# Turning row maxima and expert tokens in 32 x 32 squares on DVE, with transfers that put the squares in place

## The chip, the cores and the metric
The kernel runs on one core of a Trainium2 chip. The metric is the device time of one execution in microseconds. A run is told as the time of that core; where a profile is read, its span is the time from the first to the last instruction that the profiler saw. Before: 1392.12 us, median of 3 runs (1388.15 to 1392.15).

## The reference
One layer on a sequence of S = 2048 rows of width D = 128: a layer norm without gain, attention with 16 heads of width 64, and a mixture of 8 experts of which each token uses one. Everything is float32; Wq, Wk, Wv and Wo are drawn 8 times larger than usual, so the scores are large and the row maxima must really be subtracted.

```python
xn = layernorm(x)                                   # (1, 2048, 128)
q, k, v = xn @ Wq, xn @ Wk, xn @ Wv                 # 16 heads of 64
scores = einsum('bqhd,bkhd->bhqk', q, k) * 64**-0.5
attn = softmax(scores, axis=-1)
a = einsum('bhqk,bkhd->bqhd', attn, v).reshape(1, 2048, 1024) @ Wo + bo
expert = argmax(softmax(xn @ router_w.T))           # one of 8 for each token
h = square(relu(xn @ expert_fc[expert]))            # 128 -> 512
f = h @ expert_proj[expert].T                       # 512 -> 128
out = x + a + f
```

## The kernel before, in words
**Blocks.** The heads are taken in 8 pairs (h = 0, 1), the queries in 4 chunks of 512. A pair and a chunk make a block n, 32 in all. In a block the loop runs over 16 key tiles kt of 128. For each kt and head PE makes a scores tile of 128 keys x 512 queries in one of three PSUM banks SB: a high product (`high_scores`, L1062) and a low product on top of it (`low_scores`, L1069). Queries and keys are split in a rounded high part and the rest, so K1/Q1 hold one set of parts and K2/Q2 another. ACT takes the exponential of the tile (L619), POOL and DVE add the tiles up for the denominators (L505, L790), and PE multiplies them with V in batches of 8 key tiles (`times_v`, L1116), after kt 8 of the same block and after kt 0 of the next.

**The row maxima.** The scores tile has keys on the partitions, so a query's maximum can't be subtracted there as a per-partition number. It goes in as one more row of the product: K2 holds a row of ones at partition 64 (head 0) or 0 (head 1), and Q2 holds minus the maximum of each query at that row. The maxima come from a second set of products, queries x keys, in three PSUM banks MB (`max_unit`, L1088; 32 units for a block), each reduced by DVE over 512 keys (`maxima`, L767). They run ahead of their block: at kt 11 of block n the last unit of block n + 1 is done. DVE then reduces 4 key chunks to one and negates (`minus_max`, L779) into `nm`, 128 x 8: partition = query in its tile of 128, column = head and query tile. At kt 12 (`AT_T`) PE turns `nm` into the spare PSUM bank XB (`turn_max`, L1169), ACT copies the 8 x 128 result to `mrow` (L653), and SP copies 4 rows per head into the row of Q2 (`place_max`, DMAs from L365). The first low product of block n + 1 (kt 0, head 0) waits for this on the semaphore `d_nm`.

**The expert tokens.** Early blocks sort the tokens by expert into the DRAM tensor `sorted_x`, in 23 tiles of 128 rows. Blocks 4 to 26 do one tile each. SP loads `tok` and two weight matrices at the end of the block before (`load_tile`, L416 to L418). At kt 3 PE turns `tok` (L1037), ACT copies it to `tokT` (L697), at kt 4 PE makes the first product (`expert_up`, L1043), at kt 11 the second (L1050).

**Order.** Each engine's program is written out by hand: the same two nested loops (blocks, kt) on every engine, in which the constants `AT_...` say at which kt a job stands. Engines run their programs in order and meet in semaphores. The spare bank XB is shared by all small PE jobs in turn: `take_spare` makes each wait until the one before it was read out. All DMAs but the indirect ones are issued by SP, in its own order: in a block the K pieces (two sets of 6, in blocks n with n % 4 < 2 and n < 28; "K work"), the Q pieces (6), then `place_max`, the store of an expert result (L423) and `load_tile`. K work is also a product, an ACT copy and, for K, a DVE subtraction (`low_k`, L903) at kt 1 and 9.

Of the kernel before, what the change touches and what calls it, by code (L numbers as in the profile page):

```python
# [30 lines left out]
P = 128  # L31
# [52 lines left out]


LEAD = 8
UNITS = 2 * TB * JB
# [17 lines left out]
def layer(nc, x, wq, wk, wv, wo, bo, router_wT, fc, projT, out):  # L105


    with ExitStack() as ctx:
# [3 lines left out]
        def sem(name):  # L112
            return ctx.enter_context(nc.semaphore(name))

        def bank(name, n=1):
# [48 lines left out]
        on = osb  # L164
        mx, nm = sb("mx", [P, 2, UNITS]), sb("nm", [P, 2, 2 * TB])
        mrow = sb("mrow", [2 * TB, P], F32R)
        MB_all, SB_all = bank("MB", 3), bank("SB", 3)
# [4 lines left out]

        t_s, t_m, t_pv, t_q, t_k, t_v, t_den, t_wo, t_nm = (
            sem(f"t_{n}") for n in ("s", "m", "pv", "q", "k", "v", "den", "wo", "nm"))

        a_e, a_o, a_q, a_k, a_w, a_v, a_nm, a_den = (
            [sem("a_e0"), sem("a_e1")], *(sem(f"a_{n}") for n in ("o", "q", "k", "w", "v", "nm", "den")))

        v_m, v_nm, v_q, v_k, v_w, v_rd, v_y = (
            sem(f"v_{n}") for n in ("m", "nm", "q", "k", "w", "rd", "y"))  # L180

# [13 lines left out]

        d_tile, t_tok, t_up, t_down, a_tok, a_up, a_res, g_hid, d_res, d_back, v_back = (
            sem(n_) for n_ in ("d_tile", "t_tok", "t_up", "t_down", "a_tok", "a_up", "a_res", "g_hid", "d_res",
                               "d_back", "v_back"))
# [5 lines left out]
        d_out = sem("d_out")  # L204
        QD, KD = 6 * 16, 6 * 16

# [142 lines left out]
        with nc.Block() as block:  # L349
            @block.sync  # L350
            def _(sp):
# [53 lines left out]
                def place_max(m):  # L405
                    k = m % QS
                    wait(sp, a_nm, m.times(1, 1))
                    wait(sp, g_z, 4 + 2 * QS if m.off else 4)
                    for h in range(2):
                        copy(Q2[k][h][maxrow[h], :], mrow[h * TB:(h + 1) * TB, :], d_nm[k])  # L410

                def load_tile(r):


                    e = sp.value_load(owner_i[0:1, bass.ds(r.place(1), 1)], min_val=0, max_val=E - 1)
                    sp.dma_start(tok[:, :], sorted_x[bass.ds(r.place(P), P), :]).then_inc(d_tile, 16)  # L416
# [79 lines left out]
            def _(pool):  # L496
# [46 lines left out]
                def first():  # L543
# [10 lines left out]
                                       base=0, pattern=[[1, P]], channel_multiplier=-1)  # L554
                    pool.memset(one_e[:, :], 1.0)
                    pool.memset(gate[:, :, 1:NT], 1.0)
                    pool.memset(gate[:, :, 0:1], 0.0)
# [53 lines left out]
            def _(act):  # L611
# [35 lines left out]

                def max_rows(m):
                    wait(act, t_nm, m.times(1, 1))
                    if not (m.i is None and m.off == 0):  # L650
                        old = m - 1
                        wait(act, d_nm[old % QS], (old // QS).times(32, 32))
                    act.activation(mrow[:, :], XB[0:2 * TB, 0:P], ACT.Copy).then_inc(a_nm, 1)  # L653

                def take_o(n):
# [38 lines left out]

                def copy_tokens(r):
                    wait(act, t_tok, r.times(1, 1))
                    act.activation(tokT[:, :], XB[:, 0:P], ACT.Copy).then_inc(a_tok, 1)  # L697

                def rectify(r):
# [8 lines left out]
                def first():  # L708
                    act.wait_ge(g_i, 2)
                    act.activation(up[:, 0:1], eps[:, 0:1], ACT.Sqrt)  # L710

                    root(0)
                    split_w(Lin(0))
                    root(1)
                    turned(0)
                    turned(1)
                    root(2)
                    root(3)
                    high_q0()
                    high_k0(0)  # L720
                    high_k0(1)
                    for p in range(UNITS // 2):
                        kind, c = BETWEEN.get(p, (None, 0))
                        if kind == "t":
                            turned(c)
                            copy_k0(c - 2)
                        elif kind == "k":
                            high_k0(c)
                            copy_k0(c)
                        elif kind == "v":  # L730
                            kv("v", Lin(0), c)
                        elif kind == "q":
                            high_q(Lin(c))
                    max_rows(Lin(0))

                def one(n):
                    for kt in range(NT):
# [3 lines left out]
                        if has_tile(n):  # L741
                            if kt == AT_TOK:
                                copy_tokens(n - TILE0)
# [10 lines left out]
                        if kt == AT_DEN and not (n.i is None and n.off == 0):  # L754
                            take_sums(n - 1)
                        if kt == AT_T and before(n, NB - 1):
                            max_rows(n + 1)

# [3 lines left out]
            def _(dve):  # L762
# [13 lines left out]
                def minus_max(m):  # L776
                    wait(dve, v_m, m.times(UNITS, UNITS))
                    wait(dve, t_nm, m.times(1, -1))
                    dve.tensor_reduce(nm[:, m % 2, :], mx[:, m % 2, :].rearrange("p (a b) -> p a b", b=JB), AX.X,  # L779
                                      ALU.max, negate=True).then_inc(v_nm, 1)  # L780

                def add(n, kt):
# [102 lines left out]
                def find_owners():  # L885
# [3 lines left out]
                    dve.tensor_scalar(owner_i[:, :], owner[:, :], float(E - 1), None, ALU.min).then_inc(v_own, 1)  # L889

                def take_back(j):
                    dve.wait_ge(d_back, 16 * NT)
                    dve.wait_ge(v_y, NB - 2)
                    dve.tensor_tensor(chunk(Y, j), chunk(Y, j), chunk(back, j), ALU.add).then_inc(v_back, 1)
# [22 lines left out]
                def first():  # L917
# [17 lines left out]
                    for u in range(EARLY):  # L935
                        maxima(Lin(1), u)
                    choose()
                    for u in range(EARLY, MIDDLE):
                        maxima(Lin(1), u)

                def one(n):
                    start = n.i is None and n.off == 0
                    for kt in range(NT):
# [3 lines left out]
                        if kt == AT_NM and before(n, NB - 1):  # L947
                            minus_max(n + 1)
                        if kt in AT_KV and before(n, NB - JB):
                            kind, pair, c = kv_jobs(n)[AT_KV.index(kt)]  # L950
# [16 lines left out]
                        if n.off == NB - 1 and kt in BACK:  # L967
                            take_back(BACK[kt])
                        if kt == AT_WO:
                            if start:  # L970
# [28 lines left out]
            def _(pe):  # L999
# [165 lines left out]

                def turn_max(m):
                    take_spare(a_nm, m.times(1, 1))
                    wait(pe, v_nm, m.times(1, 1))
                    pe.transpose(XB[0:2 * TB, 0:P], nm[:, m % 2, :], ident[:, :]).then_inc(t_nm, 1)  # L1169

                def first():
# [22 lines left out]
                    for p in range(UNITS // 2):  # L1194
# [10 lines left out]
                        elif kind == "r":  # L1205
                            logits(c)
                    for u in range(EARLY):
                        max_unit(Lin(1), u)
                    turn_max(Lin(0))
                    for u in range(EARLY, MIDDLE):  # L1210
                        max_unit(Lin(1), u)
# [3 lines left out]
                def one(n):  # L1215
                    start = n.i is None and n.off == 0
                    for kt in range(NT):
# [8 lines left out]
                        if has_tile(n):  # L1226
                            if kt == AT_TOK:
                                turn_tokens(n - TILE0)
                            if kt == AT_UP:
# [7 lines left out]
                        if kt == AT_WO and not start:  # L1237
                            project(n - 1)
                        if kt == AT_T and before(n, NB - 1):
                            turn_max(n + 1)  # L1240
                        if kt == AT_DEN and not start:
# [45 lines left out]
```

## Time and profile before

| | |
|---|---|
| median of 3 runs | 1392.12 us (1388.15 to 1392.15) |
| the profiled execution | 1389.63 us |
| its span | 1387.9 us |
| mean granted TensorE clock | 0.993 |
| PE busy | 1365.8 us, 98% of the span |
| POOL busy | 1121.8 us, 81% |
| DVE busy | 1078.0 us, 78% |
| ACT busy | 735.2 us, 53% |

The profile comes from one execution. Busy time of PE counts a product from its issue to the modelled end in a pipeline, so two neighbours overlap: a 128 x 512 product has a duration of 0.39 us but the next one starts 0.23 us later. The chain of waits takes the overlap out and gives each its own share. SPq is the queue of SP: the time in which it issues a DMA. "Releaser" is the instruction or the DMA whose end lifted a wait.

### The profile page before, as it was taken

The numbers are of one execution on the slowest core, as the hardware profiler recorded it, in microseconds if no ns is written. First come the engines' busy times: TensorE is split into PE (matmuls) and PEld (weight loads), VectorE is DVE, ScalarE is ACT, GpSimd is POOL, SyncE is SP. The second block draws the span as 40 slices with busy tenths as digits, with TensorE's granted clock in tenths as the row PEclk, the third lists the DMA queues.
The fourth block names the chain that finished last, engine by engine and source line by source line (L and its number), as shares of the span: only waits on it lengthen the run. The fifth ranks groups of instructions, "written<-read, shape, count | busy, mean of one in ns | idle before, by whom it ended". The sixth has DMA issues, their size and how long they took to land.

```text
span 1387.9 us, 20006 instructions
## 1 busy us (share of the span) xinstructions
PE 1365.8 (98%) x6447; PEld 866.1 (62%) x6447; DVE 1078.0 (78%) x1468; ACT 735.2 (53%) x1316; POOL 1121.8 (81%) x908
## 2 busy tenths in 40 slices
PE   7899999999999999999999999999999999999997
PEld 4566666566665666666766666656667666656644
DVE  7987887786787767777777777778677777788877
ACT  4465455565464554554644645545546446556543
POOL 7779997777787877877878877879777788789995
PEclk8999999999999999999999999999999999999998
DMA  4241113220132201331113311123112231111000
GB/s 104 58 120 41 37 41 70 70 67 20 43 89 57 60 19 43 94 69 44 34 39 84 73 40 43 43 71 90 24 42 55 64 79 26 24 23 33 11 19 23
DMA packets 65255, 72.38 MB, mean 52 GB/s; under 512 B 9024, under 2 KB 38272, under 8 KB 65152
## 3 DMA queue, kind: packets, MB, share of 16 engines
q1 hardware_dynamic: 64128, 69.01, 20.3%
q0 software_dynamic: 1024, 2.10, 0.5%
q8 instruction: 52, 0.85, 0.2%
q14 instruction: 51, 0.42, 0.1%
HBM read 17.83 MB, written 5.11 MB: 17 GB/s over the span
## 4 chain that ended last, share of the span: by engine, by line
PE 93%; DVE 2%; POOL 1%; DMA 1%; issue 1%; SPq 1%; ACT 1%; POOLq 0%; DVEq 0%; ACTq 0%
PE OB L1116 31%; PE SB L1062 17%; PE SB L1069 16%; PE MB L1088 15%; PE XB L1153 2%; PE XB L1144 2%; PE XB L1162 2%; PE XB L1050 1%; PE XB L1043 1%; POOL acc L505 1%; DVE mx L767 1%; PE XB L1123 1%; PE XB L1125 1%; PE XB L1124 1%; DMA K<-low 1%
## 5 line engine op out<-in xcount | busy, mean ns | idle before, releaser
L505 POOL TENSOR_TENSOR acc<-acc,ex 128x512 f32<-128x512 f32 x717 | 915.9, 1304 | 99.9 <-DVE acc L790 40.4
L767 DVE TENSOR_REDUCE mx<-MB 128x1 f32<-128x512 f32 x992 | 655.9, 688 | 228.9 <-PE MB L1088 224.1
L619 ACT ACTIVATE ex<-SB 128x512 f32<-128x512 f32 x1024 | 607.2, 599 | 329.8 <-PE SB L1069 262.0
L1116 PE MATMUL OB<-ex,V 128*64 128x512 f32 x2048 | 452.7, 594 | 0.0
L1062 PE MATMUL SB<-Q,K 128*128 128x512 f32 x1024 | 421.9, 412 | 0.5 <-ACT ex L619 0.5
L1069 PE MATMUL SB<-Q,K 128*128 128x512 f32 x1024 | 399.8, 390 | 0.8 <-DMA Q<-mrow 0.8
L1088 PE MATMUL MB<-K,Q 128*128 128x512 f32 x992 | 389.1, 392 | 1.6 <-DVE mx L773 0.6
L1116 PEld LDWEIGHTS OB<-ex,V 128*64 128x64 f32 x2048 | 143.9, 137 | 284.3 <-issue 273.0
L1062 PEld LDWEIGHTS SB<-Q,K 128*128 128x128 f32 x1024 | 192.6, 188 | 96.5 <-issue 53.5
L790 DVE TENSOR_TENSOR acc<-acc,ex 128x512 f32<-128x512 f32 x179 | 205.0, 1145 | 13.5 <-ACT ex L619 1.0
L1088 PEld LDWEIGHTS MB<-K,Q 128*128 128x128 f32 x992 | 186.1, 188 | 46.7 <-DVE mx L767 5.0
L1069 PEld LDWEIGHTS SB<-Q,K 128*128 128x128 f32 x1024 | 193.1, 189 | 32.9 <-DMA Q<-mrow 1.2
L505 POOL TENSOR_TENSOR acc<-ex 128x512 f32<-128x512 f32 x63 | 79.8, 1287 | 137.6 <-ACT ex L619 137.5
L658 ACT ACTIVATE osb<-OB 128x512 f32<-128x512 f32 x32 | 19.1, 598 | 204.0 <-PE OB L1116 204.0
L908 DVE RECIPROCAL rd<-rd 128x256 f32<-128x256 f32 x62 | 104.1, 1720 | 0.0
L511 POOL TENSOR_TENSOR osb<-osb,rd 128x512 f32<-128x512 f32 x31 | 40.4, 1304 | 3.9 <-DVE rd L908 3.9
L898 DVE SCALAR_TENSOR_TENSOR low<-XB,high 128x512 fp32r<-128x512 f32 x31 | 21.4, 692 | 22.8 <-ACT high L633 22.8
L1144 PEld LDWEIGHTS XB<-wraw,xT 128*128 128x128 f32 x256 | 34.0, 195 | 3.5 <-issue 1.2
L1144 PE MATMUL XB<-wraw,xT 128*128 128x128 f32 x256 | 35.0, 281 | 0.0
L1162 PEld LDWEIGHTS XB<-wo,osb 128*128 128x128 f32 x248 | 32.4, 191 | 2.8 <-issue 0.4
L1153 PE MATMUL XB<-acc,ones 128*64 128x512 f32 x124 | 33.4, 618 | 0.0
L1162 PE MATMUL XB<-wo,osb 128*128 128x128 f32 x248 | 32.7, 275 | 0.0
(136 smaller groups left out, 608.8 us busy)
## 6 DMA issues: line engine op xcount, KB each, us to landing
Q<-high SPq DMA_DIRECT2D x124, 128.0 KB, 2.3
K<-high SPq DMA_DIRECT2D x112, 128.0 KB, 2.3
Q<-low SPq DMA_DIRECT2D x64, 128.0 KB, 2.4
K<-low SPq DMA_DIRECT2D x56, 128.0 KB, 2.3
w<-fc SPq DMA_DIRECT2D x23, 256.0 KB, 2.7
w<-projT SPq DMA_DIRECT2D x23, 256.0 KB, 3.1
sorted_x<-res SPq DMA_DIRECT2D x1, 1472.0 KB, 6.9
tok<-sorted_x SPq DMA_DIRECT2D x23, 64.0 KB, 1.7
```

The source lines that it names most:

```text
L505: pool.tensor_tensor(a[:, :], src[:, :], EX[h][ex_slot(kt)][:, :], ALU.add).then_inc(done, 1)
L619: act.activation(EX[h][ex_slot(kt)][:, :], SB[bank_of(n, 2 * kt + h)][:, :], ACT.Exp).then_inc(a_e[h], 1)
L767: dve.tensor_reduce(mx[:, m % 2, u:u + 1], MB[bank_of(m, i)][:, :], AX.X, ALU.max).then_inc(v_m, 1)
L790: dve.tensor_tensor(a[:, :], src[:, :], EX[0][ex_slot(kt)][:, :], ALU.add).then_inc(sums[0][n % 2], 1)
L908: dve.reciprocal(rd[:, cols], rd[:, cols]).then_inc(v_rd, 1)
L1062: pe.matmul(SB[bank_of(n, 2 * kt + h)][:, :], K1[par][h][:, keys], Q1[k][h][:, :], start=True, stop=False)
L1069: pe.matmul(SB[bank_of(n, 2 * kt + h)][:, :], K2[par][h][:, keys], Q2[k][h][:, :], start=False, stop=True).then_inc(t_s, 1)
L1088: pe.matmul(MB[bank_of(m, i)][:, :], Q1[k][h][:, q * P:(q + 1) * P], K1[par][h][:, c * QB:(c + 1) * QB], start=True, stop=True).then_inc(t ...
L1116: mm = pe.matmul(OB[own[h], :], V[(n // JB) % 2][:, k, own[h]], EX[h][ex_slot(k)][:, :], start=(k == 0), stop=(k == NT - 1))
L1144: mm = pe.matmul(XB[:, k * P:(k + 1) * P], xT[:, tok], wraw[pair % 2][:, 2, :], start=True, stop=True)
L1153: mm = pe.matmul(XB[own[h], :], ones[:, 0:DH], acc[h][n % 2][:, :], start=True, stop=True)
L1162: mm = pe.matmul(XB[:, q * P:(q + 1) * P], on[:, q * P:(q + 1) * P], wo_s[pair % 2][:, :], start=True, stop=True)
```

## The change
`nm` becomes 128 x 32 and `mrow` 128 x 32. `minus_max` writes columns 0 to 7 of `nm`; the others are set to zero once on POOL. DVE's transpose turns each square of 32 x 32 in place: `mrow[32 j + c, a]` = `nm[32 j + a, c]`. The 128 queries of a tile then lie in 4 groups j of 32, so each head's row of Q2 is put together by 4 DMAs (one for each j, 4 query tiles x 32 queries), 8 for a block instead of 2. The transpose on DVE stands at kt 12, the kt of PE's before.

The tokens: `load_tile` reads `sorted_x` in 4 DMAs, each of 32 partitions, so that square (j, i) of `tok` holds square (i, j) of the tile; one DVE transpose of 128 x 128 at kt 3 then gives the whole transpose `tokT`. It waits for all six DMAs of the tile and for the last use of `tokT` (`t_up`).

PE's `turn_max` and `turn_tokens` and ACT's `max_rows` and `copy_tokens` are gone with their semaphores.

```diff
+SQ = 32
-        mx, nm = sb("mx", [P, 2, UNITS]), sb("nm", [P, 2, 2 * TB])
-        mrow = sb("mrow", [2 * TB, P], F32R)
+        mx = sb("mx", [P, 2, UNITS])
+        nm, mrow = sb("nm", [P, SQ], F32R), sb("mrow", [P, SQ], F32R)
...
+        TD = (P // SQ + 2) * 16
+        QD, KD, MD = 6 * 16, 6 * 16, 2 * (P // SQ) * 16
...
                 def place_max(m):
                     k = m % QS
-                    wait(sp, a_nm, m.times(1, 1))
+                    wait(sp, v_mrow, m.times(1, 1))
                     wait(sp, g_z, 4 + 2 * QS if m.off else 4)
                     for h in range(2):
-                        copy(Q2[k][h][maxrow[h], :], mrow[h * TB:(h + 1) * TB, :], d_nm[k])
+                        row = Q2[k][h][maxrow[h], :].rearrange("o (q j a) -> o q j a", q=TB, a=SQ)
+                        for j in range(P // SQ):
+                            copy(row[:, :, j, :], mrow[j * SQ + h * TB:j * SQ + (h + 1) * TB, :], d_nm[k])
...
-                    sp.dma_start(tok[:, :], sorted_x[bass.ds(r.place(P), P), :]).then_inc(d_tile, 16)
+                    rows = sorted_x[bass.ds(r.place(P), P), :].rearrange("(i a) d -> a i d", a=SQ)
+                    for j in range(P // SQ):
+                        sp.dma_start(tok[j * SQ:(j + 1) * SQ, :].rearrange("a (i b) -> a i b", b=SQ),
+                                     rows[:, :, j * SQ:(j + 1) * SQ]).then_inc(d_tile, 16)
...
+                    pool.memset(nm[:, :].bitcast(F32), 0.0)
...
-                def max_rows(m):
-                    wait(act, t_nm, m.times(1, 1))
...
-                    act.activation(mrow[:, :], XB[0:2 * TB, 0:P], ACT.Copy).then_inc(a_nm, 1)
...
-                def copy_tokens(r):
-                    wait(act, t_tok, r.times(1, 1))
-                    act.activation(tokT[:, :], XB[:, 0:P], ACT.Copy).then_inc(a_tok, 1)
...
                 def minus_max(m):
                     wait(dve, v_m, m.times(UNITS, UNITS))
-                    wait(dve, t_nm, m.times(1, -1))
-                    dve.tensor_reduce(nm[:, m % 2, :], mx[:, m % 2, :].rearrange("p (a b) -> p a b", b=JB), AX.X,
+                    if m.off == 0:
+                        dve.wait_ge(g_i, 6)
+                    dve.tensor_reduce(nm[:, 0:2 * TB], mx[:, m % 2, :].rearrange("p (a b) -> p a b", b=JB), AX.X,
                                       ALU.max, negate=True).then_inc(v_nm, 1)
+
+                def turn_max(m):
+                    wait(dve, v_nm, m.times(1, 1))
+                    if not (m.i is None and m.off == 0):
+                        old = m - 1
+                        wait(dve, d_nm[old % QS], (old // QS).times(MD, MD))
+                    dve.transpose(mrow[:, :].bitcast(F32), nm[:, :].bitcast(F32)).then_inc(v_mrow, 1)
...
+                def turn_tokens(r):
+                    wait(dve, d_tile, r.times(TD, TD))
+                    wait(dve, t_up, r.times(1))
+                    dve.transpose(tokT[:, :], tok[:, :]).then_inc(v_tok, 1)
...
-                def turn_tokens(r):
-                    take_spare(a_tok, r.times(1, 1))
-                    wait(pe, d_tile, r.times(48, 48))
-                    pe.transpose(XB[:, 0:P], tok[:, :], ident[:, :]).then_inc(t_tok, 1)
...
                 def expert_up(r):
                     take_spare(a_up, r.times(1, 1))
-                    wait(pe, a_tok, r.times(1, 1))
+                    wait(pe, v_tok, r.times(1, 1))
...
-                        wait(pe, d_nm[k], (n // QS).times(32, 32))
+                        wait(pe, d_nm[k], (n // QS).times(MD, MD))
...
-                def turn_max(m):
-                    take_spare(a_nm, m.times(1, 1))
-                    wait(pe, v_nm, m.times(1, 1))
-                    pe.transpose(XB[0:2 * TB, 0:P], nm[:, m % 2, :], ident[:, :]).then_inc(t_nm, 1)
```

At the start, PE's first five maxima units of block 1 now follow one another; DVE turns the maxima of block 0 behind the first of them.

SP's order at the end of a block with an expert tile, before; `Q_20` and `Q_21` are the Q2 of heads 0 and 1, `w` the expert's weights, L415 reads the tile's expert:

```order
L365 DMA Q_20<-mrow 1x4x128
L365 DMA Q_21<-mrow 1x4x128
L423 DMA sorted_y<-res 128x128
L415 TENSOR_LOAD owner_i
L415 ISA x2
L416 DMA tok<-sorted_x 128x128
L417 ISA
L417 DMA w<-fc 128x512
L418 DMA w<-projT 128x4x128
```

The same place in the changed kernel:

```order
L369 DMA Q_20<-mrow 1x4x32 x4
L369 DMA Q_21<-mrow 1x4x32 x4
L433 DMA sorted_y<-res 128x128
L421 TENSOR_LOAD owner_i
L421 ISA x2
L425 DMA tok<-sorted_x 32x4x32 x4
L427 ISA
L427 DMA w<-fc 128x512
L428 DMA w<-projT 128x4x128
```

Four transfers of a quarter stand for each one before, for the maxima and for `tok`; everything behind them in SP's order keeps its place.

DVE's order in a block with K work and an expert tile, from kt 1 to kt 13, before (L767 is `maxima`, L903 `low_k`, L898 `low_q`, L779 `minus_max`, L790 the additions, L908 the reciprocals):

```order
L767 TENSOR_REDUCE mx<-MB 128x1 x2
L903 TENSOR_TENSOR low<-XB,high 128x512
L767 TENSOR_REDUCE mx<-MB 128x1 x8
L898 SCALAR_TENSOR_TENSOR low<-XB,high 128x512
L767 TENSOR_REDUCE mx<-MB 128x1 x6
L790 TENSOR_TENSOR acc<-acc,ex 128x512 x2
L908 RECIPROCAL rd<-rd 128x256 x2
L767 TENSOR_REDUCE mx<-MB 128x1 x2
L903 TENSOR_TENSOR low<-XB,high 128x512
L767 TENSOR_REDUCE mx<-MB 128x1 x4
L779 TENSOR_REDUCE nm<-mx 128x8
L767 TENSOR_REDUCE mx<-MB 128x1 x4
```

The same order in the changed kernel, first from kt 1 to kt 5 (L762 is now `maxima`, L913 `low_k`, L908 `low_q`):

```order
L762 TENSOR_REDUCE mx<-MB 128x1 x2
L913 TENSOR_TENSOR low<-XB,high 128x512
L762 TENSOR_REDUCE mx<-MB 128x1 x4
L899 STREAM_TRANSPOSE tokT<-tok 128x128
L762 TENSOR_REDUCE mx<-MB 128x1 x4
L908 SCALAR_TENSOR_TENSOR low<-XB,high 128x512
```

Then its kt 9 to kt 13 (L775 is `minus_max`):

```order
L762 TENSOR_REDUCE mx<-MB 128x1 x2
L913 TENSOR_TENSOR low<-XB,high 128x512
L762 TENSOR_REDUCE mx<-MB 128x1 x4
L775 TENSOR_REDUCE nm<-mx 128x8
L762 TENSOR_REDUCE mx<-MB 128x1 x2
L785 STREAM_TRANSPOSE mrow<-nm 128x32
L762 TENSOR_REDUCE mx<-MB 128x1 x2
```

The transpose of the maxima stands behind the two reductions of kt 12, that of the tokens behind the four of kt 2 and 3.

## Rows read from the trace of the kernel before

**Rows 1.** The page: busy time by engine, and the chain by engine.

```profile
PE 1365.8 (98%) x6447; PEld 866.1 (62%) x6447; DVE 1078.0 (78%) x1468; ACT 735.2 (53%) x1316; POOL 1121.8 (81%) x908
...
PE 93%; DVE 2%; POOL 1%; DMA 1%; issue 1%; SPq 1%; ACT 1%; POOLq 0%; DVEq 0%; ACTq 0%
```

**Rows 2.** Stretches: length, busy of PE, PEld, DVE, ACT, POOL, granted clock, DMA.

```profile
12.00:16.40 4.40, 2.93 (x10) 1.53 (x10) 3.52 (x15) 4.32 (x10) 1.66 (x2) 1.00 0.00 0
16.40:26.60 10.20, 10.15 (x32) 6.06 (x32) 8.25 (x9) 6.05 (x11) 6.74 (x6) 0.50 0.61 142
40.00:50.00 10.00, 6.83 (x20) 3.17 (x20) 9.83 (x19) 4.24 (x7) 4.28 (x5) 1.00 0.01 2
60.00:1375.00 1315.00, 1313.93 (x6223) 830.56 (x6223) 1024.11 (x1356) 705.06 (x1261) 1075.79 (x856) 1.00 0.21 51
```

**Rows 3.** The chain of waits, at kt 12: start, share, what.

```profile
324.62 0.11 PE XB L1169
```

**Rows 4.** Groups: line, engine, out<-in, count | busy us, mean ns | idle before.

```profile
L1169 PE MATMUL XB<-ident,nm 128*8 128x128 f32 x32 | 8.7, 272 | 1.0 <-DVE nm L779 0.9
L1037 PE MATMUL XB<-ident,tok 128*128 128x128 f32 x23 | 6.2, 271 | 0.0
L779 DVE TENSOR_REDUCE nm<-mx 128x8 f32<-128x32 f32 x32 | 6.0, 186 | 1.1
L862 DVE COPY w<-XB 128x128 f32<-128x128 f32 x1 | 0.3, 291 | 0.0
```

**Rows 5.** Timeline from block 6 to block 7: start, length, engine, what [idle before].

```profile
323.96 2.89 DVE L767 TENSOR_REDUCE mx<-MB 128x1 f32<-128x512 f32 x4 [0.67 <-PE MB L1088]
...
325.19 1.36 SPq L365 DMA_DIRECT2D Q<-mrow  x2
...
329.81 0.39 PE L1069 MATMUL SB<-Q,K 128*128 128x512 f32 x1
```

**Rows 6.** Timeline, token need: blocks without (298) and with K work (256).

```profile
298.65 4.24 DVE L767 TENSOR_REDUCE mx<-MB 128x1 f32<-128x512 f32 x6 [0.90 <-PE MB L1088]
...
302.00 1.05 PE L1043 MATMUL XB<-tokT,w 128*128 128x128 f32 x8
...
256.79 3.68 DVE L767 TENSOR_REDUCE mx<-MB 128x1 f32<-128x512 f32 x6
...
259.58 1.05 PE L1043 MATMUL XB<-tokT,w 128*128 128x128 f32 x8
```

**Rows 7.** SP's issues by line: duration ns min/median/max; last, L365's DMAs to landing.

```profile
L365 SPq DMA_DIRECT2D Q<-high x124: 461/597/612, 30.8 to 1279.7; - x124
...
L365 SPq DMA_DIRECT2D Q<-mrow x64: 573/632/722, 42.4 to 1332.6; - x64
...
L416 SPq DMA_DIRECT2D tok<-sorted_x x23: 326/332/338, 200.7 to 1136.5; - x23
...
DMA to landing us min/median/max: 2.2/2.3/3.8
```

**Rows 8.** Timeline around the first low products of blocks 0, 1 and 31.

```profile
42.40 1.40 SPq L365 DMA_DIRECT2D Q<-mrow  x2
...
44.87 0.50 PE L1069 MATMUL SB<-Q,K 128*128 128x512 f32 x1 [0.76 <-DMA Q<-mrow]
...
41.58 1.88 DVE L767 TENSOR_REDUCE mx<-MB 128x1 f32<-128x512 f32 x3
...
75.44 2.60 DVE L767 TENSOR_REDUCE mx<-MB 128x1 f32<-128x512 f32 x4
...
80.10 0.39 PE L1069 MATMUL SB<-Q,K 128*128 128x512 f32 x1
...
1339.18 0.39 PE L1069 MATMUL SB<-Q,K 128*128 128x512 f32 x1
```

**Rows 9.** Timeline, start of block 30: SP's maxima and PE's first low product.

```profile
1294.02 1.30 SPq L365 DMA_DIRECT2D Q<-mrow  x2
...
1298.62 0.39 PE L1069 MATMUL SB<-Q,K 128*128 128x512 f32 x1
```

More of the change, by code:

```diff
@@ L169, in layer @@
         OB, XB = bank("OB"), bank("XB")
[L173 to L180, printed above, removed]
+        t_s, t_m, t_pv, t_q, t_k, t_v, t_den, t_wo = (
+            sem(f"t_{n}") for n in ("s", "m", "pv", "q", "k", "v", "den", "wo"))
+        a_e, a_o, a_q, a_k, a_w, a_v, a_den = (
+            [sem("a_e0"), sem("a_e1")], *(sem(f"a_{n}") for n in ("o", "q", "k", "w", "v", "den")))
+        v_m, v_nm, v_mrow, v_q, v_k, v_w, v_rd, v_y = (
+            sem(f"v_{n}") for n in ("m", "nm", "mrow", "q", "k", "w", "rd", "y"))
         sums = [[sem(f"sum{h}_{k}") for k in range(2)] for h in range(2)]
@@ L193, in layer @@
         d_sort = [sem(f"d_sort{k}") for k in range(2)]
-        d_tile, t_tok, t_up, t_down, a_tok, a_up, a_res, g_hid, d_res, d_back, v_back = (
-            sem(n_) for n_ in ("d_tile", "t_tok", "t_up", "t_down", "a_tok", "a_up", "a_res", "g_hid", "d_res",
+        d_tile, v_tok, t_up, t_down, a_up, a_res, g_hid, d_res, d_back, v_back = (
+            sem(n_) for n_ in ("d_tile", "v_tok", "t_up", "t_down", "a_up", "a_res", "g_hid", "d_res",
                                "d_back", "v_back"))
@@ L204, in layer @@
         d_out = sem("d_out")
-        QD, KD = 6 * 16, 6 * 16
+        TD = (P // SQ + 2) * 16
+        QD, KD, MD = 6 * 16, 6 * 16, 2 * (P // SQ) * 16
         def unit(n, kt, h):
@@ L646, in kv @@
                                        ACT.Copy).then_inc(a_v, 1)
-                def max_rows(m):
-                    wait(act, t_nm, m.times(1, 1))
-                    if not (m.i is None and m.off == 0):
-                        old = m - 1
-                        wait(act, d_nm[old % QS], (old // QS).times(32, 32))
-                    act.activation(mrow[:, :], XB[0:2 * TB, 0:P], ACT.Copy).then_inc(a_nm, 1)
                 def take_o(n):
@@ L733, in first @@
                             high_q(Lin(c))
-                    max_rows(Lin(0))
                 def one(n):
@@ L741, in one @@
                         if has_tile(n):
-                            if kt == AT_TOK:
-                                copy_tokens(n - TILE0)
                             if kt == AT_UP:
@@ L755, in one @@
                             take_sums(n - 1)
-                        if kt == AT_T and before(n, NB - 1):
-                            max_rows(n + 1)
                 schedule(act, first, one, lambda: take_o(Lin(NB - 1)))
@@ L936, in first @@
                         maxima(Lin(1), u)
+                        if u == 0:
+                            turn_max(Lin(0))
                     choose()
@@ L948, in one @@
                             minus_max(n + 1)
+                        if kt == AT_T and before(n, NB - 1):
+                            turn_max(n + 1)
                         if kt in AT_KV and before(n, NB - JB):
@@ L968, in one @@
                             take_back(BACK[kt])
+                        if has_tile(n) and kt == AT_TOK:
+                            turn_tokens(n - TILE0)
                         if kt == AT_WO:
@@ L1206, in first @@
                             logits(c)
[L1207 to L1210, printed above, removed]
+                    for u in range(MIDDLE):
                         max_unit(Lin(1), u)
@@ L1226, in one @@
                         if has_tile(n):
-                            if kt == AT_TOK:
-                                turn_tokens(n - TILE0)
                             if kt == AT_UP:
@@ L1238, in one @@
                             project(n - 1)
-                        if kt == AT_T and before(n, NB - 1):
-                            turn_max(n + 1)
                         if kt == AT_DEN and not start:
```

## The prediction, made before the changed kernel ran

> **What bounds the kernel now.** I read the engine totals, the chain of waits and what PE waited for first. PE is busy 98% of the span and 93% of the chain is PE [rows 1]. From 60 to 1375 us PE is busy 1313.93 of 1315 us at full granted clock [rows 2], so in the 32 blocks there is no slack on PE at all: what leaves PE's row comes off the time, and whatever holds PE up goes on top, whole. The one DMA wait that PE shows is for the row maxima in Q2, once, 0.76 us, ahead of block 0 [rows 8]. So the question for every later block is how long before PE asks for that row it has landed.
>
> **What leaves PE.** The chain gives the maxima's transpose 0.11 us of PE's own time [rows 3]; the tokens' has the same 128 columns and the same duration. The 0.27 us shown as mean duration includes the pipeline's depth. There are 32 and 23 of them [rows 4], 55 x 0.11 = 6.1 us. The spare PSUM bank is never waited for in those places in the block region, so nothing more is won there. The ACT copies that go are off the path: ACT is 53% busy [rows 1] and keeps up with PE.
>
> **What comes in on DVE.** A transpose of 128x32 for the maxima and one of 128x128 for the tokens. The trace before has no DVE transpose. The nearest rows are the 128x32 reduction at 0.186 and the 128x128 copy at 0.291 us [rows 4]; I take these, allow half of them below and double above. The Trainium skill (page "VectorE: DVE Perf Modes", section "The three transpose paths") gives 311 ns for DVE and 390 ns for TensorE for 128x128 in bf16, and its rules section sends whole 128x128 transposes to TensorE. On PE's own row the cost here is 0.11 us, so the trace doesn't bear out that a DVE turn saves the difference of those two; with 311 ns the sum would change by 0.2 us.
> The order puts the maxima's transpose behind the two reductions of kt 12. In a middle block four reductions follow one another from 323.96 at 0.69 each [rows 5], the second ends at 323.96 + 1.38 = 325.34, the transpose at 325.53, and SP can start at 325.58 instead of 325.19 [rows 5]: 0.39 us later. What is queued behind on DVE are reductions for PE's ring of three MB banks; 0.19 us there is covered, since DVE sits idle for PE in every block (0.67 us just before these four).
> For the tokens: PE needs tokT at 302.00 in a block without K work, 0.11 sooner once the transpose is gone, so 301.89. DVE's four reductions from 298.65 at 0.71 (six in 4.24) end at 301.47, plus 0.29 and 0.05 makes 301.81: in time. In a block with K work six take 3.68 from 256.79, the fourth ends at 259.24, the turned tile stands at 259.58, needed at 259.58 - 0.11 = 259.47 [rows 6]: 0.11 late. 12 of the 23 tiles (blocks 4, 5, 8, 9, ... 24, 25) are of that sort: 1.3 us, call it 1.5. The token tile's four DMAs stand in SP's order right behind the maxima and the result's store, so they end 5.6 us later at most (4.1 for six more maxima issues, 1.1 for three of their own at 0.33, 0.4 for the start), still before the block of the need begins on PE, and kt 3 lies behind a 7 us batch of value products. They, and the two weight loads behind them, cost PE nothing.
>
> **What comes in on SP, which decides.** The maxima now go out in 8 DMAs instead of 2, each of 4 x 32 instead of 4 x 128 elements. SP's row for this transfer is 573/632/722 ns for one issue, though it moves only 2 KB; the 128 KB transfers on the same line take 597 [rows 7]. So size does not set it, and cutting the transfer in four does not make each part cheaper. Two of them take 1.36 us [rows 5], a pitch of 0.68. Eight make 5.44 us. From the last issue's end to PE's release: ahead of block 0 SP ends at 42.40 + 1.40 = 43.80 and PE starts at 44.87, 1.07 us [rows 8].
> Middle block: 325.58 + 5.44 + 1.07 = 332.09. PE asks at 329.81 [rows 5], 0.11 sooner without its transpose: 329.70. PE stands still for 2.39 us. Behind the waiting product stand all of PE's further products in order; nothing goes ahead. Ahead of block 7 (325.19 to 329.81) as of block 30 (1294.02 to 1298.62) SP starts 4.60 to 4.62 us before PE asks [rows 5, 9], with K work too, where SP comes free 0.5 us before its turn. Block 2 has 0.3 less of it but, its DVE being ready sooner, starts about as much sooner. So 29 boundaries (blocks 2 to 30) x 2.39 = 69.3 us.
> Block 1: DVE's reductions from 75.44 at 0.65 make 76.74, so SP starts at 76.98 and the row has landed at 83.49; PE asks at 80.10 - 0.11 = 79.99 [rows 8]: 3.5 us. Block 0: first reduction from 41.58 takes 0.63, transpose until 42.40, SP from 42.45, landed at 48.96 against 44.87 now: 4.1 us. Block 31: a half batch of PE's value products lies between, SP starts near 1331.4, landed 1338.0, PE asks at 1339.18 [rows 8]: nothing.
> Sum: 69.3 + 3.5 + 4.1 + 1.5 - 6.1 = +72 us. On the profiled execution's 1389.63 us that is 1462. The median of the runs shown, 1392.12, is 2.5 us above that execution, which lies between the lowest and the highest of them; I leave the number at 1462.
>
> **Bounds.** Issue: the cheapest issue of this line is 461 ns, pitch 0.50, 8 in 4.0 us; the wait falls to 0.95 in a middle block and the sum to 72 - 31 x 1.44 = +27 (1417). The dearest maxima issue, 722 ns, has a pitch of 0.76: + 31 x 0.64 = +20. Landing: 1.70 us here from the start of an issue, 2.3 for the large ones of that line [rows 7]: up to +19. Transposes at double price: 31 x 0.19 and 23 x 0.29 at most, +13. Together at the top about 1513. I take 0.68 because it is the same kind of transfer to the same place.
> The Trainium skill (page "DMA: Bandwidth & Descriptors", section "Issuing engines are not separate DMA queues") says that the sequencer's time to initiate a DMA is usually small relative to the DMA itself. In this trace the issue is 0.63 us of 1.70 for 2 KB, so the trace doesn't agree for such small transfers. Were the issue negligible, the six added DMAs would be hidden and the time would come out at the fast rival's below.
>
> **Rivals.**
> 1. The clock falls in the new waits. For it: from 12 to 16.4 us PE was busy 2.93 of 4.4 us, and from 16.4 to 26.6 the granted clock was 0.50 although PE was busy throughout, which costs half of 10.2 us, 5.1 us. Against: between 40 and 50 PE was busy only 6.83 of 10 us and the clock stayed at 1.00 [rows 2]. Neither row settles what one gap of 2.39 us does. If a third of the 31 waits bring that on, +53: 1515; if all do, +158: 1620.
> 2. Faster: the eight issues fit. It needs 325.58 + 8 x pitch + 1.07 to be under 329.70, a pitch under 0.38 us. For it: SP's issues of the token tile take 0.33 [rows 7], so such a pitch exists on this queue. Against: these start from DRAM; of the maxima's line none is under 0.46, 2 KB or 128 KB. Then 6.1 us less and 1.5 for the tokens: 1385 (with a hidden token turn 1383.5). At a pitch of 0.38 to 0.40 it would come out as no change.
> 3. Issues cheaper than now, but above 0.4 us, as transfers of 128-byte pieces: 1395 to 1440.
>
> **How the numbers follow.** Forecast as summed, with the bounds on pitch and landing near it (1441 to 1500): 0.62. Clock: 0.17, half of that above 1530. Cheaper issues: 0.14. Fits on SP: 0.04. No change: 0.03. A measurement here tells about 0.3% (4 us) from none. Faster 0.04, same 0.03, slower 0.93. The range leaves out the fast rival, no change, the lowest third of the cheap issues and the upper half of the clock: 1405 to 1530; the likeliest case alone has 1441 to 1500.
>
> **What would show it.** Right: on PE a wait for the DMA Q<-mrow in 31 blocks of 2 to 3 us, some 75 us in all; 256 issues of Q<-mrow on SP in runs of 5.2 to 5.6 us; PE's busy share down to 93%; DVE transposes of about 0.2 and 0.3 us; ACT and POOL busy as before. PE's row has 55 matmuls less, and the pieces between the waits are as long as now with the granted clock at 1.00. Wrong: an issue of the small pieces well off 0.63 us (the wait moves by 8 times the difference); a granted clock of 0.50 behind the waits; DVE backlog that delays the maxima; or a tile wait at the expert's first product beyond 0.2 us.

## The result, and the profile after

The changed kernel takes 1460.99 us (median of 4, 1459.58 to 1462.84), the kernel before 1390.71 (median of 4): a ratio of 1.0508, 95% interval 1.0485 to 1.0532. It is 70 us slower; 1462 was forecast. The profiled execution took 1462.84 us, its span is 1461.1 us.

From the page of the changed kernel, its busy times and the chain by engine, to set against [rows 1]:

```profile
PE 1377.1 (94%) x6392; PEld 862.9 (59%) x6392; DVE 1042.2 (71%) x1523; ACT 726.8 (50%) x1261; POOL 1113.3 (76%) x909
...
PE 75%; SPq 11%; DVE 5%; DMA 4%; issue 3%; POOL 1%; ACT 1%; POOLq 0%; DVEq 0%; ACTq 0%
```

PE has 55 products less and yet more busy time, since some ran at half clock (below). SP's queue, 1% of the chain before, is now 11%, and DMA 4%. What PE waited for (instruction, line, releaser: us in total, times, longest):

```profile
PE SB L1080 <- DMA Q<-mrow: 62.9, 31, 4.1
```

31 waits, none in block 31, as the forecast had them. The rows that answer to [rows 4] and [rows 7] (groups by line: L785 and L899 are DVE's two transposes; then from the view of SP's DMA issues, min/median/max in ns):

```profile
L899 DVE STREAM_TRANSPOSE tokT<-tok 128x128 f32<-128x128 f32 x23 | 6.9, 300 | 0.0
L785 DVE STREAM_TRANSPOSE mrow<-nm 128x32 f32<-128x32 f32 x32 | 6.4, 201 | 0.0
```

```profile
L369 SPq DMA_DIRECT2D Q<-mrow x256: 572/573/722, 40.9 to 1411.1; - x128
```

A quarter of the bytes costs SP nearly the same time. One middle boundary (ahead of block 12) in the timeline, to be read against [rows 5]:

```profile
571.15 1.39 DVE L762 TENSOR_REDUCE mx<-MB 128x1 f32<-128x512 f32 x2 [0.68 <-PE MB L1099]
572.46 0.20 DVE L785 STREAM_TRANSPOSE mrow<-nm 128x32 f32<-128x32 f32 x1
...
572.68 5.05 SPq L369 DMA_DIRECT2D Q<-mrow  x8
...
576.66 0.39 PE L1073 MATMUL SB<-Q,K 128*128 128x512 f32 x1
578.78 0.50 PE L1080 MATMUL SB<-Q,K 128*128 128x512 f32 x1 [1.74 <-DMA Q<-mrow]
```

DVE has turned at 572.66, SP issues from 572.68 to 577.73, 1.05 us later the row is there and PE starts. Without the wait PE would have started 0.23 us behind 576.66, at 576.89: it lost 1.89 us. The 1.74 in the brackets is less because it counts from the modelled end of the product before.

The whole block shows it best. ACT copies the output bank once a block, always released by PE, so the distance of two copies is a block's time. Here blocks of the same kind (no K work, with a tile), first before, then changed:

```profile
508.60 0.60 ACT L658 ACTIVATE osb<-OB 128x512 f32<-128x512 f32 x1 [6.66 <-PE OB L1116]
551.27 0.60 ACT L658 ACTIVATE osb<-OB 128x512 f32<-128x512 f32 x1 [6.36 <-PE OB L1116]
```

```profile
542.80 0.60 ACT L662 ACTIVATE osb<-OB 128x512 f32<-128x512 f32 x1 [6.67 <-PE OB L1127]
587.28 0.60 ACT L662 ACTIVATE osb<-OB 128x512 f32<-128x512 f32 x1 [6.37 <-PE OB L1127]
```

42.67 against 44.48 us. I call these block times from here on.

The granted clock also fell. Stretches of the changed kernel (columns as in [rows 2]):

```profile
400.20:403.60 3.40, 3.40 (x9) 0.93 (x10) 3.18 (x6) 0.90 (x2) 1.12 (x1) 0.56 0.49 118
403.60:420.00 16.40, 16.37 (x77) 10.57 (x74) 8.05 (x15) 8.76 (x16) 9.51 (x8) 0.99 0.25 60
803.40:806.80 3.40, 3.40 (x10) 0.99 (x10) 2.96 (x5) 0.60 (x1) 0.70 (x1) 0.51 0.51 111
```

A mean of 0.56 means that 0.4 us of the first stretch were still at full clock: the fall begins at 400.6, 1.6 us behind the wait that ended at 398.99. The third stretch, from 803.4, follows this wait:

```profile
802.21 0.50 PE L1080 MATMUL SB<-Q,K 128*128 128x512 f32 x1 [2.46 <-DMA Q<-mrow]
```

There are seven such falls to half speed (1.2 of 2.4 GHz) in the block region, of 3.4 us each, from 86.6, 130.9, 175.3, 264.0, 400.6, 803.4 and 1291.5 us, and one around the wait for block 0 (42.2 to 52.4). Each begins near the end of a wait for `Q<-mrow`, from 0.3 us before to 1.6 us behind it. None lies between 60 and 1375 us before [rows 2].

### The profile page after: what moved, and what is told of

The parts are those of the page before. It is cut to its first block, busy times and chain, and to the rows that moved or that the text cites. A ratio compares the mean times of both kernels' runs of the same rounds, so it can differ in the third digit from the quotient of the medians.

```text
span 1461.1 us, 20096 instructions
## 1 busy us (share of the span) xinstructions
PE 1377.1 (94%) x6392; PEld 862.9 (59%) x6392; DVE 1042.2 (71%) x1523; ACT 726.8 (50%) x1261; POOL 1113.3 (76%) x909
## 4 chain that ended last, share of the span: by engine, by line
PE 75%; SPq 11%; DVE 5%; DMA 4%; issue 3%; POOL 1%; ACT 1%; POOLq 0%; DVEq 0%; ACTq 0%
PE OB L1127 30%; PE SB L1080 12%; PE SB L1073 12%; PE MB L1099 11%; SPq L369 10%; DMA Q<-mrow 4%; DVE mx L762 3%; PE XB L1164 2%; PE XB L1155 2%; PE XB L1054 2%; PE XB L1061 1%; POOL acc L515 1%; PE XB L1134 1%; PE XB L1136 1%; PE XB L1135 1%
## 5 line engine op out<-in xcount | busy, mean ns | idle before, releaser
L762 DVE TENSOR_REDUCE mx<-MB 128x1 f32<-128x512 f32 x992 | 653.9, 684 | 343.6 <-PE MB L1099 342.5
L1127 PE MATMUL OB<-ex,V 128*64 128x512 f32 x2048 | 460.2, 602 | 0.0
L795 DVE TENSOR_TENSOR acc<-acc,ex 128x512 f32<-128x512 f32 x179 | 168.5, 942 | 11.8 <-issue 0.5
L908 DVE SCALAR_TENSOR_TENSOR low<-XB,high 128x512 fp32r<-128x512 f32 x31 | 21.4, 691 | 20.3 <-ACT high L644 20.3
```

The costliest lines, as they stand in the source:

```text
L762: dve.tensor_reduce(mx[:, m % 2, u:u + 1], MB[bank_of(m, i)][:, :], AX.X, ALU.max).then_inc(v_m, 1)
L795: dve.tensor_tensor(a[:, :], src[:, :], EX[0][ex_slot(kt)][:, :], ALU.add).then_inc(sums[0][n % 2], 1)
L1127: mm = pe.matmul(OB[own[h], :], V[(n // JB) % 2][:, k, own[h]], EX[h][ex_slot(k)][:, :], start=(k == 0), stop=(k == NT - 1))
```

## The experiments

Times are medians; "before" was measured along with each group: 1388.15 us with numbers 1 to 4, 1388.47 with 6, 7, 8 and 10, 1388.62 with 5 and 9. Ratios are to that. Block times and clocks come from the one profiled execution of each.

**1. Tokens only.** The kernel before with the changed `load_tile`, `turn_tokens` and `expert_up`, the maxima as they were.

```diff
-                    pe.transpose(XB[:, 0:P], tok[:, :], ident[:, :]).then_inc(t_tok, 1)
+                    dve.transpose(tokT[:, :], tok[:, :]).then_inc(v_tok, 1)
```

> Only the tokens are turned on DVE, the maxima go by PE, ACT and 2 DMAs as before. Theory (the maxima's issues on SP are the cost): 23 x 0.11 = 2.5 us come off PE, and in the 12 tile blocks with K work the tile's turn on DVE comes some 0.4 us late for the expert's first product, as in the profile of the changed kernel (5.1 us in 12 waits): about 1391 + 2.5 = 1393 us, at most one wait of PE for Q<-mrow, ahead of block 0. Rival (the token part carries a good part of the 70 us, by its small DMAs or by DVE): 1405 us or more.

Measured: 1387.52 us, ratio 0.9989 (0.9972 to 1.0006). Alone the token part costs nothing that can be told from none, so the loss is in the maxima. The 5 us that I expected here were overestimated: the rows called "issue" stand before the expert's weight load, and products cover part of that time. Block times show what the late tile costs: +0.13 us in blocks with K work (42.32 for 42.19), -0.16 in the others (42.52 for 42.68). With 0.11 saved in both, a late tile costs 0.24 us, 12 times, or 2.9 us in all. The rest of the 5 us between the 1393 expected and the time measured is mostly that I had started from 1391, where the kernel before took 1388.15 here.

**2. Maxima only.** The changed kernel, with tokens by PE and ACT again.

```diff
-                    dve.transpose(tokT[:, :], tok[:, :]).then_inc(v_tok, 1)
+                    pe.transpose(XB[:, 0:P], tok[:, :], ident[:, :]).then_inc(t_tok, 1)
```

> Only the maxima are turned on DVE and placed by 8 DMAs, the tokens are turned by PE as before. Theory: the waits for Q<-mrow and the clock's falls stay as in the changed kernel, so 1461 + 2.5 (PE's token turns back) - 5.1 (no late tile) = 1458 us, 31 waits. Rival (the two parts collide on SP or DVE): clearly under 1450 us.

Measured: 1467.63 us, ratio 1.0558 (1.0528 to 1.0588); 31 waits of 62.3 us and again seven falls of the clock behind block 0. The parts don't collide. It is 6.6 us above the changed kernel where 3 below was expected; the intervals of the two ratios just touch, and the spans of the two profiles differ by 4.1 us. Some 2 of the 9 us missed are the overestimate of number 1, which this expectation also used. The granted clock was lower in its executions (means of 0.978 to 0.985, for 0.985 to 0.989 in the changed kernel), but how much of the rest that makes is not shown.

**3. Eight DMAs in the kernel before.** PE and ACT turn; only the transfer is cut up.

```diff
-                        copy(Q2[k][h][maxrow[h], :], mrow[h * TB:(h + 1) * TB, :], d_nm[k])
+                        row = Q2[k][h][maxrow[h], :].rearrange("o (q j a) -> o q j a", q=TB, a=SQ)
+                        for j in range(P // SQ):
+                            copy(row[:, :, j, :], mrow[h * TB:(h + 1) * TB, j * SQ:(j + 1) * SQ], d_nm[k])
```

> The kernel before, with PE's and ACT's turn, but the 2 DMAs of the maxima are cut in 8 of 4 x 32. Theory (the number of issues on SP is the cost): SP starts as before, 8 issues at 0.63 us and 1.05 us to land end 6.1 us later, against 4.62 us until PE asks: 1.5 us in each of 29 middle blocks, about 2.7 in block 1 and 3.7 in block 0, 50 us in all, and some falls of the clock on top: 1440 to 1455 us. Rival (the DVE turn and its later start are the cost): 1391 to 1400 us.

Measured: 1449.44 us, ratio 1.0428 (1.0397 to 1.0459); 31 waits of 46.2 us. DVE's transpose isn't needed for the loss; six more issues on SP cost 61 us, with PE still turning. A middle block costs 1.67 us more than before (44.34 for 42.67), in the changed kernel 2.06 more than with two DMAs. The difference of 0.39 us is the later start on SP that was forecast for DVE's place at kt 12.

**4. Two of the eight DMAs.** The changed kernel, but only the first piece of each head's row is written: three quarters of the queries have no maximum subtracted.

```diff
-                        for j in range(P // SQ):
+                        for j in range(1):
```

> The changed kernel with only the first piece of each head's maxima written, 2 DMAs of 8; three quarters of the queries have no maximum subtracted. Theory: with 2 issues the row has landed 2.0 us before PE asks: no wait but the one ahead of block 0, granted clock 1.00 in all blocks, PE's 6.1 us are won and the tokens' 5 us lost: 1388 to 1391 us. Rival (the small pieces land late, or DVE's turn is late, whatever their number): waits of 1 us and more remain, 1420 us or more.

Measured: 1381.37 us, ratio 0.9928 (0.9907 to 0.9949); one wait, of 0.6 us, the clock at 1.00 from 27 us to the end of the last block. It is 7 us under the 1388 to 1391 expected, partly because the tokens' 5 us of number 1 were counted here too and because the kernel before took 1388.15 and not 1391. Both transposes are on DVE, and the time is 7 us under before: this is the change without its price. A middle block with a tile takes 42.42 us (506.89 to 549.31) for 42.67, which is what two products of 0.11 us on PE are worth.

**5. Six of the eight**; for a quarter of the queries no maximum is subtracted.

```diff
-                        for j in range(P // SQ):
+                        for j in range(3):
```

> The changed kernel with the first three pieces of each head's maxima written, 6 DMAs of 8; for a quarter of the queries no maximum is subtracted. Theory (each issue past the slack costs its pitch): with 8 a middle wait costs 2.05 us of block time, two issues at 0.64 less make it 0.77, 31 waits: 1381 (two of eight) + 31 x 0.77 + about 2.5 for blocks 0 and 1 = 1407 us, with no or one fall of the clock after block 1. Rival (the wait does not follow the count: one late landing, all or nothing): above 1440, or as with two of eight.

Measured: 1412.14 us, ratio 1.0159 (1.0133 to 1.0185), 5 us above the expected number. Its timeline, SP and then PE:

```profile
505.67 3.82 SPq L369 DMA_DIRECT2D Q<-mrow  x6
```

```profile
510.54 0.50 PE L1080 MATMUL SB<-Q,K 128*128 128x512 f32 x1 [0.51 <-DMA Q<-mrow]
```

The block takes 43.25 us. So 2, 6 and 8 issues make 42.42, 43.25 and 44.48: the last two issues cost 1.23 us, twice the pitch of 5.05 / 8 = 0.63, and the first ones nothing until the slack is used up. A single late landing would not follow the count. Against two of the eight a block costs 0.83 us more, not 0.77, and blocks 0 and 1 together 3.7, not 2.5; the rest of the 5 us is in a few longer blocks.

**6. Turn at kt 11.** DVE's transpose right behind `minus_max`.

```diff
                         if kt == AT_NM and before(n, NB - 1):
                             minus_max(n + 1)
+                            turn_max(n + 1)
...
-                        if kt == AT_T and before(n, NB - 1):
-                            turn_max(n + 1)
```

> The changed kernel, DVE turns the maxima right behind minus_max at kt 11 instead of behind the two reductions of kt 12. Theory (start of the 8 issues + 8 pitches + landing against the time at which PE asks): where SP is free, the start comes 2.05 us sooner, as much as a middle wait costs (2.05 us a block by the block times of both profiles), so 0 to 0.3 us is left; ahead of blocks that follow K work SP is free only 0.9 us sooner, 1.15 us left, 14 times 16 us. Block 0 stays (7 us with its clock). About 1400 to 1410 us, and no fall of the clock but the one at block 0. Rival (the number of DMAs in flight, not when they start, makes the row late): above 1440.

Measured: 1430.49 us, ratio 1.0278 (1.0242 to 1.0314). Better, and 20 us worse than expected. Where SP is free the expectation holds: a middle block takes 42.53 us, 0.1 above the version with two DMAs. Ahead of blocks that follow K work 43.55, or 1.35 left, since SP is still issuing K pieces. Five times one of those pieces took over a microsecond too long; here ahead of block 6, where DVE was ready at 299.10:

```profile
298.06 2.47 SPq L369 DMA_DIRECT2D K<-high  x2
300.58 0.60 SPq L369 DMA_DIRECT2D K<-low  x1
301.29 5.03 SPq L369 DMA_DIRECT2D Q<-mrow  x8
```

(the same two issues take 1.24 elsewhere). Three falls of the clock remain in the blocks, and in the profiled execution the granted clock was 0.50 from 29.4 to 56.7 us, and the first copy of the output bank came 5 us later than in the changed kernel. These I had not counted.

**7. LEAD 12.** The maxima run 4 kt further ahead, and SP places them ahead of the second K pieces; the turn stays right behind `minus_max`.

```diff
-LEAD = 8
+LEAD = 12
-AT_DEN, AT_KV, AT_Q, AT_WO, AT_NM, AT_T = 8, (1, 9), 5, 13, 11, 12
+AT_DEN, AT_KV, AT_Q, AT_WO, AT_NM, AT_T = 8, (1, 9), 5, 13, 9, 12
...
-                    if spread[1]:
-                        spread_k(*spread[1][1:])
                     if before(n, NB - 1):
                         place_max(n + 1)
+                    if spread[1]:
+                        spread_k(*spread[1][1:])
```

> The changed kernel with the maxima units 4 kt instead of... LEAD 12 for 8, so their last unit stands at kt 9, minus_max and the turn at kt 9, and SP places the maxima ahead of the second K pieces. Theory: 6 us more for the eight issues, no wait in any block but block 0; what is left of the change is PE's 6 us won, some 2 us lost by late tiles, and block 0's 7 us: 1390 to 1395 us, no clock fall behind block 1. Rival (K pieces delayed by the maxima make ACT and PE wait): above 1400.

Measured: 1389.04 us, ratio 1.0000 (0.9985 to 1.0016). One wait is left, 3.6 us, at block 0, with half clock from 43.3 to 53.5 us; all eight DMAs are issued in every block. A middle block takes 42.42 us, as with two of eight. The loss in the middle blocks was a matter of place, not of the transfers as such.

**8. LEAD 12, MIDDLE 11, tokens at kt 2.** As 7, and block 0 begins after 11 instead of 5 maxima units of block 1.

```diff
-AT_TOK, AT_UP, AT_DOWN = 3, 4, 11
+AT_TOK, AT_UP, AT_DOWN = 2, 4, 11
...
-        EARLY, MIDDLE = 3, 5
+        EARLY, MIDDLE = 3, 11
```

> As the kernel with LEAD 12, and: the tokens are turned at kt 2 instead of kt 3, and PE makes 11 maxima units of block 1 before block 0 instead of 5 (these fill the wait for block 0's maxima). Theory: the late tiles' 2 us and most of block 0's 7 us go too: 1383 to 1387 us, faster than both kernels. Rival (DVE, which reduces each unit in 0.69 us, is the bound there, so that the wait only moves): as the kernel with LEAD 12 within 2 us.

Measured: 1382.34 us, ratio 0.9950 (0.9933 to 0.9966): no wait for Q<-mrow, and faster than both kernels. Blocks with K work now take 41.93 us (42.19 before), the others 42.41 (42.67): twice and a bit the 0.11 us of a transpose. At the start PE now waits for DVE instead, 3.1 us in three waits, and the granted clock is still 0.50 there, from 40.7 to 47.6 us.

**9. The same lead in the kernel before.** PE turns both; maxima and start as in 8, while SP's order of maxima and K pieces and the tokens' kt 3 stay.

```diff
-LEAD = 8
+LEAD = 12
...
-AT_DEN, AT_KV, AT_Q, AT_WO, AT_NM, AT_T = 8, (1, 9), 5, 13, 11, 12
+AT_DEN, AT_KV, AT_Q, AT_WO, AT_NM, AT_T = 8, (1, 9), 5, 13, 9, 12
...
-        EARLY, MIDDLE = 3, 5
+        EARLY, MIDDLE = 3, 11
```

> The kernel before (PE turns both) with LEAD 12, minus_max at kt 9 and 11 maxima units of block 1 before block 0, as the faster kernel had them. Theory: what made that one faster than the kernel before is the 6 us that left PE; the earlier maxima alone give nothing where no wait was, and at block 0 at most 1.5 us: 1386 to 1389 us. Rival (the gain came from the order, not from the turns): 1382 us, as that kernel.

Measured: 1392.08 us, ratio 1.0022 (1.0008 to 1.0036), 3 us above what I expected: the order alone loses a little, at the start and the end; its middle blocks take 42.67. Against it, number 8 is 9.7 us faster, with DVE's turns and SP's order of maxima and K pieces changed together. The block times of the two profiles place it: 0.27 us in each of 23 blocks with a tile, 6 us in all, and 1 us at the start. Another 1.5 us are two blocks of number 9 that took 0.7 and 0.9 us longer than others of their kind, for a reason not shown. So turning on DVE is worth at least the 6 us once its transfers are out of the way.

**10. Filler.** The changed kernel; while PE waits for the maxima of blocks 1 to 30 it runs 8 products into the spare bank that nobody reads.

```diff
+FILL = 8
...
                     if kt == 0 and h == 0:
+                        if 0 < n.off < NB - 1:
+                            wait(pe, v_y, n.times(1, -1))
+                            for _ in range(FILL):
+                                pe.matmul(XB[:, :], K1[par][0][:, keys], Q1[k][0][:, :], start=True, stop=True)
                         wait(pe, d_nm[k], (n // QS).times(MD, MD))
```

> The changed kernel, in which PE runs 8 products that nobody uses (into the spare bank) while it waits for the maxima ahead of blocks 1 to 30: 8 x 0.23 = 1.84 us of the 2.05. Theory of the clock (it falls because PE stands still there, each fall costs 2.1 us of block time): the falls of blocks 1 to 30 go, the waits stay as long in sum: 1461 - 7 x 2.1 = 1446 us, waits shown for Q<-mrow under 10 us. Rival (the falls come from elsewhere, or cost nothing): 1461 us or more.

Measured: 1455.5 us, ratio 1.0479 (1.0443 to 1.0515). The clock over its whole block region:

```profile
60.00:1440.00 1380.00, 1373.05 (x6415) 871.46 (x6415) 988.69 (x1410) 698.39 (x1211) 1069.77 (x858) 1.00 0.20 49
```

In the profiled execution no fall is left but the one at block 0, although PE does 240 products more. The median is 5.5 us lower, but the intervals of the two ratios overlap (1.0485 to 1.0532 for the changed kernel), so the evidence is the clock in the profile and not the time. Together with number 3, where 28 waits of 1.3 us brought no fall, it says that the falls came from PE standing still. Each costs 1.5 to 1.7 us of block time (46.18 for 44.51 with the filler, 44.96 for 43.40), half of its 3.4 us, and not the 2.1 that I expected: I had laid the whole length of the block around 264 us to the clock, but with the filler it is almost as long (46.15 for 46.27).

## Why the prediction was right

The mechanism was the predicted one: eight issues on SP outlast its slack, and PE waits in 31 blocks. That the number was only 1 us off is partly luck, since terms missed in opposite directions. Block times of four profiles split it: before, two of eight (one short wait), filler (waits, no falls behind block 0) and the changed kernel.

| from the start to ACT's last copy of O | forecast | measured |
|---|---|---|
| work moved off PE, late tiles | -4.6 | -5.7 (before to two of eight) |
| waits for the maxima | +76.9 | +71.9 (two of eight to filler) |
| clock, blocks 0 to 31 | 0 | +8.7 (filler to changed) |
| sum | +72 | +75 |

The span grew by 73.2; the last 1.6 us come back behind the last copy, a stretch that I didn't follow up.

Of the 71.9 us, 65.7 are in blocks 2 to 30, where 69.3 were forecast. A plain wait of 2.05 us would make 59.5 there, 10 under the forecast; another 6 us are in blocks that took longer than that (some waits were 2.2 to 2.5 us, behind a late issue or a late landing), for which the forecast had no term. These 6 us and the 8.7 of the clock made up for the waits that were sized too large and for an early start (below).

- **What leaves PE.** 0.11 us for each product held: a block with a tile and no K work became 0.25 us shorter. With K work it stayed at 42.19, since the late tile cost 0.22 to 0.24 us and not 0.11, or 2.6 to 2.9 us instead of 1.5. The 5.7 us in the table look better than that because two blocks of the profile before (from 423.04 and 551.27) took 0.7 and 1.1 us longer than others of their kind; without them it is 3.9 for 4.6 forecast.
- **The page on transposes.** The Trainium skill (page "VectorE: DVE Perf Modes", section "The three transpose paths") has 311 ns on DVE for 390 on TensorE, for 128x128 in bf16; here DVE took 300 ns in float32. The rule for kernel authors on the same page that sends whole 128x128 transposes to TensorE is not borne out in this kernel, where PE is full: number 8 beats number 9.
- **DVE.** 201 and 300 ns, estimated 186 and 291. The start on SP came 0.02 us behind DVE's end. Its place behind the reductions of kt 12, priced at 0.39 us a block, is what the changed kernel has beyond number 3, whose SP starts behind PE's turn and ACT's copy as before.
- **SP's pitch, the mis-sized term.** It was 0.63 us, not 0.68: of a pair the first issue is the dearer, and pairs were all that the trace before had. 8 x 0.05 = 0.4 us in each middle block. The wait cost 2.05 instead of 2.39 us: 0.1 of it is PE's restart, which I hadn't counted (the product behind the wait holds PE 0.34 us for 0.23).
- **Landing.** 1.05 us in most blocks, 1.07 forecast. Ahead of blocks 1 to 3, 5, 10 and 16 it was 1.1 to 1.7. Ahead of blocks 14 and 17 SP began 0.5 and 0.8 us behind DVE's turn instead, since an issue of a K piece had taken 1.8 us.
- **The clock, the first rival.** It was right in part: seven of 31 waits brought a fall behind block 0, but of 1.6 us each and not 5.1. It had been priced from the only fall in the trace, whose 10.2 us are three times as long as those behind a short wait.
- **Blocks 0, 1, 31.** The first low products of blocks 0 and 1 in the changed kernel, to be read against [rows 8]:

```profile
47.01 0.79 PE L1080 MATMUL SB<-Q,K 128*128 128x512 f32 x1 [4.07 <-DMA Q<-mrow]
85.64 0.50 PE L1080 MATMUL SB<-Q,K 128*128 128x512 f32 x1 [3.47 <-DMA Q<-mrow]
```

Block 0 starts 2.1 us later than before and not 4.1. The pitch makes 0.4 of the difference. The other 1.6 are luck: `minus_max` already ran at 39.92 instead of 41.47, ahead of all that the change touches. The half clock from 16.4 to 26.6 us [rows 2] is missing in this execution, as in the profile of number 1, where it ran at 38.86; in that of number 4, which has it, it ran at 41.53. The half clock around this wait cost little: the high product that started at 50.82 before starts at 53.06 now, 2.2 us later, hardly more than the wait itself. Block 1 waited 3.5 us, as forecast. Together with the fall from 86.6 us that makes the first copy of the output bank 7.3 us later (95.75 for 88.47). Block 31: no wait, as forecast.
- **The fast rival** failed at its own condition: a pitch under 0.38 us. 0.57 us is the least that an issue of 0.5 KB took. The third, cheaper issues, holds for 0.05 us.

That six issues more on SP cause the waits is shown (3, 4, 5), and that an earlier start takes them away (6, 7). That the waits cause the falls is shown by one profiled execution of number 10. Why an issue on SP now and then takes a microsecond longer is open.

## What to carry to other kernels

Before a transfer is cut in pieces, count issues, not bytes: between tiles in SBUF each piece held the issuing queue for about 0.6 us, whether it moved 128 KB, 2 KB or 0.5 KB. Loads from DRAM held it for less, but again not by size: 0.33 us for the 64 KB of `tok`, 0.43 us as the median of its quarters. The sum of the issues has to fit into the slack between the producer and the consumer. If it doesn't, start the chain earlier before giving up the change: the same eight DMAs cost a middle block nothing once the maxima ran 4 key tiles further ahead and went out ahead of the K pieces. On an engine that is busy 98% of the time, a short stop can also cost what the clock takes behind it, here 1.6 us for each fall.

## What the runs showed of the hardware that I had not expected

- Waits on a PE that was otherwise always busy brought a granted clock of 0.50 for 3.4 us, and more often the longer they were. In the changed kernel it fell with 2 of the 22 waits of 1.7 to 2.1 us and with 5 of the 8 longer ones. Together with numbers 2, 3, 5 and 6, and with block 0 left out, it is 6 of 47 and 14 of 23, and none of 69 waits of up to 1.4 us.
- The start differs between executions: the stretch of half clock from 16.4 to 26.6 us [rows 2] is missing in the changed kernel:

```profile
14.00:30.00 16.00, 13.86 (x65) 8.43 (x65) 14.81 (x21) 10.70 (x19) 10.25 (x9) 1.00 0.49 115
```

- A transpose of float32 on DVE took about as long as other operations of that size: 128x128 in 0.300 us (a copy 0.291), 128x32 in 0.201 us (a reduction 0.186).
- SP's issues of the same transfer are not alike: in the runs of eight the first took 690 ns, the second 622 and the others 573, so pairs have a median of 628 (number 4). Single issues of K and Q pieces took up to 1837 and 2194 ns in the changed kernel, for 597 as a rule.
